# The next image's first group norm placed in the layer-norm and offset stages, and one half of the shifted copies issued from ScalarE's queue

## The reference

```python
    x = x + _L0_conv_ref(_gn(x), ...)   # 1x1 query, 256x256 channel attention, softmax, times query
    x = x + _L1_conv_ref(_gn(x), ...)   # per-pixel 3x3 kernels made from the image, applied to a projection of it
    x = x + _L2_conv_ref(_gn(x), ...)   # depthwise 3x3, batch norm, relu, prune, 1x1, batch norm, relu, prune
    x = x + _L3_conv_ref(_gn(x), ...)   # deformable sampling, below
```

```python
    xproj = inp @ in_w + in_b
    x1 = conv(x, dw_w)                  # depthwise 3x3
    x1 = gelu(layer_norm(x1 + dw_b))    # over the channels of each pixel
    offset = x1 @ off_w + off_b         # 16 groups x 9 taps x 2
    mask = softmax((x1 @ mask_w + mask_b).reshape(N, H, W, 16, 9), -1)
    out = _dcnv3_core(xproj, offset, mask)  # 9 bilinear samples of xproj a pixel and group, weighted by mask
    out = out @ out_w + out_b
```

## Time and profile before

| | us |
|---|---|
| median of 3 runs | 5162.05 |
| lowest and highest | 5159.5, 5181.4 |
| the profiled execution, its own time | 5161.16 |
| its span | 5159.3 |
| mean granted TensorE clock | 0.851 of full speed |

### The profile page before, as it was taken

The page is one execution under the profiler, slowest core; times in us unless marked ns, Lnnn a source line. Parts: engine busy times, 40 slices in busy tenths (PEclk is TensorE's granted clock), DMA queues, the critical chain, the costliest instruction groups (busy, mean ns, idle before and its releaser), DMA issues.

```text
span 5159.3 us, 53812 instructions
## 1 busy us (share of the span) xinstructions
PE 3691.0 (72%) x20052; PEld 2031.9 (39%) x20052; DVE 3666.5 (71%) x4996; ACT 1749.6 (34%) x2417; POOL 416.9 (8%) x245
## 2 busy tenths in 40 slices
PE   5566677787777777777777777777777777678443
PEld 2232334444343444444344443434444343444332
DVE  4288786868778686877868687786868778686732
ACT  1233333334333333433333243333333333333310
POOL 0010101001010000101000010101101010100001
PEclk9778797988979799897989889797998889898676
DMA  9324345364544536454453645445364544536463
GB/s 421 114 54 94 94 107 147 80 166 122 131 122 109 142 85 163 122 144 116 113 146 75 160 122 132 121 105 146 83 166 122 129 124 102 148 84 158 125 156 91
DMA packets 648677, 663.34 MB, mean 129 GB/s; under 512 B 467872, under 2 KB 549792, under 8 KB 644448
## 3 DMA queue, kind: packets, MB, share of 16 engines
q1 hardware_dynamic: 644432, 652.45, 48.7%
q0 software_dynamic: 3984, 7.45, 0.5%
HBM read 280.10 MB, written 275.78 MB: 108 GB/s over the span
## 4 chain that ended last, share of the span: by engine, by line
PE 34%; DVE 31%; ACT 12%; DMA 8%; SPq 8%; issue 6%; POOL 2%; DVEq 0%; POOLq 0%; ACTq 0%
PE ps L696 6%; DVE work L945 6%; PE ps L553 5%; DVE work L936 4%; DVE spread L1230 4%; DVE partial L1219 4%; PE ps L675 4%; DMA mout<-xp 4%; SPq L503 4%; DMA out<-res 3%; DVE spread L1219 3%; PE ps L779 2%; SPq L458 2%; PE ps L743 2%; PE ps L580 2%
## 5 line engine op out<-in xcount | busy, mean ns | idle before, releaser
L1230 DVE TENSOR_TENSOR spread<-spread,partial 128x1344 f32<-128x1344 f32 x384 | 598.2, 1558 | 13.2
L1219 DVE TENSOR_TENSOR partial<-haty,hatx 128x1344 f32<-128x1344 f32 x384 | 596.6, 1554 | 5.0
L621 PE MATMUL ps<-work,w2x 128*128 128x512 f32 x1152 | 535.1, 604 | 75.9 <-DVE work L936 64.8
L743 PE MATMUL ps<-spread,cst 128*128 128x448 f32 x576 | 338.6, 675 | 314.4 <-DVE spread L1230 138.8
L1219 DVE TENSOR_TENSOR spread<-haty,hatx 128x1344 f32<-128x1344 f32 x288 | 445.6, 1556 | 150.8 <-ACT qx L1385 64.0
L1467 ACT ACTIVATE partial<-spread 128x128 f32<-128x128 f32 x288 | 124.8, 433 | 1133.2 <-PE ps L745 1050.3
L936 DVE SCALAR_TENSOR_TENSOR work<-ps,cols,qx 128x512 f32<-128x512 f32 x576 | 405.5, 747 | 15.8 <-PE ps L621 5.5
L1503 POOL TENSOR_TENSOR small<-small,cst 128x2 f32<-128x2 f32 (+1 forms) x80 | 212.3, 2654 | 2496.8 <-DVE small L888 2496.8
L553 PE MATMUL ps<-xp,wts 128*128 128x512 f32 x640 | 335.8, 673 | 101.0 <-ACT xp L1345 72.4
L621 PEld LDWEIGHTS ps<-work,w2x 128*128 128x128 f32 x1152 | 207.1, 189 | 383.2 <-DVE work L936 227.1
L1248 DVE SCALAR_TENSOR_TENSOR res<-ps,cols,res 128x256 f32<-128x256 f32 x128 | 56.0, 479 | 402.8 <-PE ps L780 402.3
(11 more groups left out here) (254 smaller groups left out, 6066.6 us busy)
## 6 DMA issues: line engine op xcount, KB each, us to landing
band<-taps_dram SPq DMA_DIRECT2D x512, 384.0 KB
taps_dram<-partial SPq DMA_DIRECT2D x1280, 48.0 KB
work<-xp SPq DMA_DIRECT2D x128, 396.0 KB, 6.7
near<-img_dram SPq DMA_DIRECT2D x256, 128.0 KB
qx<-xp SPq DMA_DIRECT2D x64, 396.0 KB, 4.7
img_dram<-band SPq DMA_DIRECT2D x6, 4096.0 KB, 43.0
taps_dram<-band SPq DMA_DIRECT2D x6, 4096.0 KB, 87.1
om_now<-om SPq DMA_DIRECT2D x32, 576.0 KB, 4.8
```

The source lines that it names most:

```text
L621: pe.matmul(bank(4 + i % 4), w2x[:, half, tap, :], tr[:, h * HALF:(h + 1) * HALF], start=True, stop=True).then_inc(s_w, 1)
L743: pe.matmul(bank(1, inner), ident, parts[:, 1, :], start=True, stop=False)
L1219: return build(vec.tensor_tensor(o, haty[:, :, 3 * i:3 * i + 3, :].rearrange("p e j a -> p j e a"), cells, ALU.mult))
L1230: done = build(vec.tensor_tensor(total, total, spare, ALU.add))
```

## The change

- A fourth stream, `first`, takes the whole of gn0 out of side. In round b it norms image b+2, one round before side works on that image. Its five keys FIRST_AT lie between 70.05 and 73.52, inside om: moments on VectorE, group_stats on TensorE (now in another part of the bank, `OM + TG // 8`), the variance, rstd on GpSimd, the norm on ScalarE.
- The reach of the points moves from qx to work, and their codes from qx to the tile big. GpSimd's write of the codes therefore also waits until the projected image has been stored (s_imgw), and ScalarE's copies of the transposed query into big wait until the signs have been counted (s_counted).
- first_ranks and its row move on TensorE from the end of side to taps (key RANKS_AT).
- `replicate` on SyncE keeps half k=1. A new `replicate` on ScalarE issues the four copies of half k=0, directly behind the norm of that half.
- All tables of keys are replaced. build 0 and, in some places, SUM and KEEP stand in other places than before.

The core of the diff:

```diff
+FIRST_AT = [70.053, 71.549, 71.605, 72.913, 73.521]
...
+        reach = work[:, K * N:K * N + POINTS]
+        code = big[:, :, :].rearrange("p t c -> p (t c)")[:, 0:POINTS]
...
+                if b + 2 < batches:
+                    streams.append(first(b + 2))
...
-                for turn, k in enumerate(HALVES):
-                    sp.wait_ge(s_norm, f * 8 + 2 * i + turn + 1)
-                    for j in range(4):
-                        ...
-                        sp.dma_start(copies(k, j)[0:3 * QUAD, :], windows).then_inc(s_rep[k], 16)
+                k = HALVES[0]
+                sp.wait_ge(s_norm, f * 8 + 2 * i + 1)
+                for j in range(4):
+                    sp.dma_start(copies(k, j)[0:3 * QUAD, :], windows(k, j)).then_inc(s_rep[k], 16)
...
+            def first(f):
+                yield FIRST_AT[1]
+                group_stats(f * 2 + 1, 4, OM + TG // 8)
...
-                yield STEP["gn0"] + 2
-                group_stats(f * 2 + 1, 4)
...
+            def first(f):
+                yield FIRST_AT[0]
+                ve.wait_ge(s_x, f * 16 + 16)
+                yield from moments(lambda k, h: x[:, k, h * HALF:(h + 1) * HALF], K, f * 5 + 1, FIRST_AT[2], OM + TG // 8)
...
+            def first(f):
+                yield FIRST_AT[4]
+                for k in HALVES:
+                    wait(ac, s_rep[k], 2 * f * COPIES)
+                yield from group_norm(f, 0, FIRST_AT[4] - 3)
...
+            def replicate(f, i):
+
+                k = HALVES[1]
+                ac.wait_ge(s_norm, f * 8 + 2 * i + 2)
+                for j in range(4):
+                    ac.dma_start(copies(k, j)[0:3 * QUAD, :], windows(k, j)).then_inc(s_rep[k], 16)
...
-                yield from group_norm(2, STEP["L2"])
+                yield from group_norm(f, 2, STEP["L2"])
+                replicate(f, 2)
...
-                yield from group_norm(3, STEP["L3"])
+                yield from group_norm(f, 3, STEP["L3"])
+                replicate(f, 3)
...
+            def first(f):
+                yield FIRST_AT[3]
+                rstd(f, 1, K)
```

More of the change, by code:

```diff
@@ L678, in side @@
                     yield STEP["om"] + (t + 1) // 2
-                yield STEP["sparse"] + 1
-                wait(pe, s_res, 4 * (f - 2) + 3)
-                first_ranks(0, f)
-                pe.wait_ge(s_counted, f + 1)
-                pe.matmul(ps[0:1, 2, 16:16 + P], runs[:, 0:1], ident, start=True, stop=True).then_inc(s_row, 1)
             def depthwise(f, stage, k):
@@ L727, in far_points @@
             def far_points(n):
-                yield STEP["gn0"] + 2.1
+                yield RANKS_AT[0]
+                wait(pe, s_res, 4 * (n - 2) + 3)
+                first_ranks(0, n)
+                pe.wait_ge(s_counted, n + 1)
+                pe.matmul(ps[0:1, 2, 16:16 + P], runs[:, 0:1], ident, start=True, stop=True).then_inc(s_row, 1)
+                yield LIST_AT
                 point_list(0, n)
-                yield TURNED_AT
+                yield TURNED_AT[0]
                 turn_values(0, n)
-                yield MIXED_AT
+                yield MIXED_AT[0]
                 mix_values(0, n)
@@ L781, in sample @@
                     mm.then_inc(s_o, 1)
-            run(side, taps, sample)
+            run(first, side, taps, sample)
             pe.wait_ge(s_total, batches)
@@ new lines, in first, with moments @@
+            def first(f):
+                yield FIRST_AT[0]
+                ve.wait_ge(s_x, f * 16 + 16)
+                yield from moments(lambda k, h: x[:, k, h * HALF:(h + 1) * HALF], K, f * 5 + 1, FIRST_AT[2], OM + TG // 8)
+            def moments(src, c, stat, start, at=0):
+                for k in range(c):
+                    for h in range(2):
+                        last = vec.bn_stats(stats[:, k, h, :], src(k, h))
+                link(last)
+                for k in range(c):
+                    last = vec.bn_aggr(small[:, 2 * k:2 * k + 2], stats[:, k, :, :].rearrange("p a b -> p (a b)"))
+                link(last)
+                mean, var = small[:, 0:2 * c:2], small[:, 1:2 * c:2]
+                link(vec.tensor_tensor(small[:, 8:8 + c], mean, mean, ALU.mult))
+                vec.tensor_tensor(var, var, small[:, 8:8 + c], ALU.add).then_inc(s_gstat, 1)
+                yield start
+                ve.wait_ge(s_gsum, stat)
+                link(vec.tensor_copy(small[:, 12:12 + 2 * c], bank(7, 2 * c, at)))
+                variance(c)
@@ L1072, in take @@
                     vec.memset(small[0:1, 62:63], 0.0)
-                then(vec.max(out=taken[:, 8:16], in_=qx[:, 0:POINTS]))
+                then(vec.max(out=taken[:, 8:16], in_=reach))
                 vec.scalar_tensor_tensor(out=real, in0=taken, scalar=0.5, in1=cst_("ones"), op0=ALU.is_gt, op1=ALU.mult,
@@ L1562, in nothing @@
                 yield END
-            run(side, taps, nothing)
+            run(first, side, taps, nothing)
             po.wait_ge(s_stored, batches * 4 * 16)
```

170 lines of the change are left out of this document (81 added, 89 removed).

## The result

The changed kernel took 5219.54 us (median of 4 runs, 5213.68 to 5223.12), the kernel before, run beside it, 5163.03 (5159.5 to 5181.4): a ratio of 1.0103, 95% interval 1.0086 to 1.0121. It is slower by 1%, some 56 us. The profiled execution took 5223.12 us with a span of 5221.3, against 5161.16 and 5159.3.

The account below looks back on a forecast made before the run. No engine is full; each stage's last hand-over sets the time. L2, L3 and ln: +2.0 for 16 images, +32 us; om and head: +3.4 for 15, +51; together +83 on 5161.2, giving 5244 us, range 5095 to 5310.

Parts of the forecast that it names:

- Head: Start of the round to L0's update of x: removed gn0 work already hidden in the wait for hats; +1 us, ends -5 and +4.
- L2: Copies before L2's depthwise: two queues share full DMA engines, so half 1 lands later; +5.5 us, ends 0 and +7.3.
- L3: Copies and projection before L3's depthwise: copies start sooner, but ScalarE's issues delay the projection; -0.7 us, ends -3.0 and +2.5.
- ln: Layer norm after L3's second depthwise: mean goes ahead of PROJECT, so variance matmuls start sooner; -2.8 us, ends -3.6 and -1.5.
- om: Offset matmuls to exponential: gn0's variance waits for group_stats and delays evictions, maximum and table load; +2.4 us, upper end +6.
- Rival A: Two queues don't disturb half 1: L2 0, L3 -3.0, ln -2.8; faster, 5119 us; chance 0.24.
- Rival B: Head shortens because VectorE has no idle behind the hats: -5 in place of +1; 5154 us; chance 0.16.
- rival C: x lands late and ScalarE's issues take 7.9 us: om +6, L3 +2.5; 5349 us; chance 0.10.

## Why the prediction was right, and where not

The sign and the range held, the time came 25 us below the forecast of 5244. The steps one by one:

- **Head**, +1 against +1.4: right, and for the reason given. gn0 was hidden in the wait for the hats; back there it costs nothing that can be told. VectorE's work behind the hats, 59.7 us in the forecast, is 59.41; its idle time there was 8.4 us before, and in the changed kernel it is 64.72 - 59.41 = 5.3:

```profile
1514.30:1579.02 64.72, 51.68 (x262) 31.64 (x266) 59.41 (x104) 16.79 (x31) 5.97 (x5) 0.87 0.49 103
```

- **L2**, the mechanism right, the term mis-sized: +5.5 against +3.3. From first issue to first depthwise I had 15.4 us, and the round shown has 15.35. That agreement is partly luck: this round is one of the two longest of the twelve, and where half 1 really was the seventh of eight it took 16.3. In the mean the first depthwise starts only 4.4 us later against the norm (14.7 for 10.3), and it then takes 5.7 us where it had taken 6.8, at a higher granted clock, as the windows above show. Why the clock was higher there more often I do not know. By the Trainium skill ("DMA: Bandwidth & Descriptors", section "Issuing engines are not separate DMA queues") the engines' DMAs interleave on the same 16 DMA engines; the trace agrees, with a later half 1 and a DMA share of 0.97 at 228 GB/s for two queues and 0.95 at 220 for one.
- **L3**, -0.7 against +2.6: the step that failed. I saw that ScalarE's issues would hold the flat copies, and took them at 4.8 us, from SyncE's four issues into an empty queue. With the DMA engines full they took 6.65, near the row of 7.41 that I had as the upper end: +1.9. And I let the first projection run in 3.72 us; after 7.5 us without a matmul it ran at a granted clock of 0.58 and took 6.41: +2.7. Together these are the 4.5 us or so by which the first depthwise came later than forecast after the norm of half 1 (22.5 against 18.1). 1.9 us came back, since both depthwise halves took 10.3 us where I had 12.15: the 6.95 of the earlier trace rows ran at a granted clock of 0.75, the 5.24 here at 1.00. So the round shown is 1.9 us longer than before and not 0.7 shorter; in the mean it is 2.6, just outside the ends of -3.0 and +2.5.
- **ln**, -2.8 against -4.8, outside the ends of -3.6 and -1.5: mechanism right, too small. The variance matmuls begin at D + 8.7 in the round shown (forecast 8.8), but then take 3.46 us at a granted clock of 1.00, where the earlier trace rows has 5.72 for them, at 0.63; I had counted nothing for that. That the mean first is worth 2 us by itself is shown. Of the other 2.8 some 2 are read off the timelines, not tested alone: the SUM of 2.05 us that stands ahead of the PROJECT in the kernel with the mean first stands behind the variance matmuls in the changed one, whose variance begins 2.05 us sooner after D in the mean (8.66 for 10.71). The rest is open.
- **om**, +2.4 against +2.1: the sum right, a part of the way wrong. I costed the moments at nothing and the wait for group_stats at everything. In the chain it is the moments that hold the evictions, and group_stats waits for them; rstd took 0.70 us, not the 1.93 that I started from, and the norm ended 1 us after the subtraction. That x would be 0 to 2 us in time did not follow from my numbers (issue 8 us ahead of O, 10.6 to land and moments at O + 8 give 5.4); it came out at 1.1, since the issue was only 1.6 us ahead of O.
- **Rival A** is excluded: the queues share. **Rival B** (no idle behind the hats) did not come. Of **rival C** one half came in its size though not by its 7.9 us, L3 at +2.6 where it had +2.5; the other, the late x, lay one step behind: as soon as L3 is faster, x is late, at a price of 4 to 7 us an image. The limit given for A, 2.3 us in L2, is 2.6 by its own terms, where 16 x (2.6 - 5.8) + 51 comes to 0.

The forecast's errors, -2.2 in L2, +3.3 in L3 and -2.0 in ln, partly cancel. The net +3.8 is less well founded than the agreement of 25 us suggests. L2, L3 and ln share one cause of error: I priced each group of matmuls by what it had taken before, and that length went with the granted clock, which the new order changed.

## What to carry to other kernels

In this kernel the copies already filled the DMA engines, and a second issuing queue made none of them faster; what counted was that those needed first went first, and that ScalarE, which issued the others, was held with everything behind it in its program. Issued at a point where ScalarE had nothing urgent behind it and half 1 was well under way, the same copies cost nothing and spared SyncE's time. Check all three before you give copies to another engine: the share of the DMA engines, the order, and what stands behind the issues. Work moved into a stage brings its inputs' deadlines along: gn0 in om needed x 9.8 us after the first offset matmul instead of 33, and a load at the end of a queue then decided what a faster L3 was worth. The length of a group of matmuls is no constant: look up its granted clock before you carry it into a sum. Before a step is moved out of a busy stretch, look whether it lies in a wait there; if it does, moving it gains nothing there.

## What the runs showed of the hardware

- Four DMA issues of 396 KB each held ScalarE for 4.77 us when half 1 had landed before them, and for 6.65 us (L3) and 6.72 us (L2) when SyncE's copies were on their way beside them.
- Two queues were kinder to half 1 than strict alternation on one: 14.7 us against 17.5 in the mean from norm to depthwise. 1.1 of these 2.8 us are SyncE's wait for the norm of the second half in the alternating kernel; the rest is open.
- The same 16 projection matmuls took 6.41 us at a granted clock of 0.58, behind 7.5 us without a matmul, and 3.72 at 1.00; 48 depthwise matmuls 6.95 at 0.75 and 5.25 at 1.00; 32 variance matmuls 5.72 at 0.63 and 3.46 at 1.00. In L3 a wait of TensorE was so paid once as a wait and again as a slower stretch behind it. In L2 it was not: half 1 came 4.4 us later and the depthwise behind it ran faster in the mean.
